# A two-layer perceiver block on one core: where the second half's state-space decays and scan inputs are computed, and the order of the work behind the first layer's attention

## The chip, the cores and the metric

The kernel runs on one core of a Trainium2 chip. The time is the device time of one launch in microseconds (us), as the median of several runs. The core has a matrix engine (TensorE, in the rows PE; PEld is its loading of weights), a vector engine (VectorE, DVE), an activation engine (ScalarE, ACT), a general one (GpSimd, POOL) and a queue that issues transfers (SyncE, SP). They run side by side and meet at semaphores: each takes its instructions strictly in the order in which they are written, so that one waiting instruction holds up everything behind it on its engine.

## What is computed

Two sequences ("halves", b = 0 and 1) of 128 tokens with 256 features pass through six residual steps, each behind a layer norm. The change lies in steps 1 and 2 and the beginning of steps 3 and 4.

```python
x = x + L0_xattn(ln(x), ctx, ctx)       # 16 heads over 2048 keys
x = x + L0_attn(ln(x), ...)             # state-space scan, 16 states per feature
x = x + L0_ffn(ln(x), ...)              # router, low-rank experts ("lora")
x = x + L1_xattn(ln(x), ctx, mask)      # one head over the same 2048 keys
x = x + L1_attn(ln(x), ...)             # 16 heads, compressed and local keys
x = x + L1_ffn(ln(x), ...)              # 8 experts

# the scan of step 2, for each feature d, state n, token t
A      = -exp(A_log)                    # (d, n)
dt     = softplus(x_proj_dt)            # (t, d)
A_bar  = exp(dt[t, d] * A[d, n])        # the decays
u      = dt[t, d] * x[t, d] * B[t, n]   # the scan's input
h[t]   = A_bar * h[t-1] + u
y[t,d] = sum_n h[t, d, n] * C[t, n] + D[d] * x[t, d]
```

## The kernel before, in words

The program is written by hand: each engine has its own list of calls, whose order is the schedule. Everything stays in the core's memory; only weights, contexts and masks are loaded.

Step 1 is a double loop over eight groups of four heads (g = 0 to 3 for the first half, 4 to 7 for the second) and 16 chunks of keys (c). Work of the first half's later steps is put between its pieces by tables named `beside`, one for each engine, keyed by group and chunk. So the first half's scan lies inside the second half's attention, and the second half's scan lies behind it. The semaphore names say what was done: `x_done0` and `x_done1` count the residual steps of a half.

The state space step of one half goes like this. TensorE transposes the normed x (`x_to_columns`, L784) and ScalarE copies it out (`transposed_x`, L503). TensorE projects the step sizes (`step_sizes`, L873), ScalarE copies them (`copy_z`, L543), VectorE takes their magnitude (`step_magnitude`, L1363), ScalarE forms exp and log (L548, L551), VectorE makes dt and dt*x (`step_and_input`, L1368 and L1370, semaphore `dtx_done`). TensorE makes B and C (`state_maps`, L882), VectorE splits them into three bf16 parts (`split_maps`), TensorE spreads each row over 128 partitions (`spread`, L897) in eight pieces of four rows for the second half, and ScalarE copies these out (`bc_copy`, L558, semaphore `bc_sb`); pieces 0 to 3 are B, 4 to 7 are C. The states of 128 features times 16 states times 128 tokens are a tile of 128x2048, and there are two of them for a half (h = 0, 1). For each: exponent dt*A (`decay_exponent`, L1392, on VectorE for the second half), exp (`decay_exp`, L563), input (`state_input`, L394, on GpSimd), scan (L1401), product with C (`read_states`, L1407, semaphore `hc_done`), and a sum over the states in 16 matmuls against the identity (`sum_states`, L905; semaphore `y_ps` when both are done). `add_states` (L1413 to L1416) adds it to x.

Around this lie: `key_mask` (L1468), which turns the loaded mask of 4096 keys into a row of one partition for step 4 and waits for two transfers (mask and bias) that SyncE issues once the first half's `read_states` are both done; `tables` (L1489 to L1499), small products of the rotation tables for step 5; `scores3`, the first half's scores of step 4 (L949, four matmul groups of 512 keys); `max3` (L1473), their maximum; `exp3` (L582); `p3_to_columns` (L960, 16 transposes); `outputs3` (L968, 16 chunks of keys); `add3` (L1482); and `lora_products` (L914, L917), the second half's first matmuls of step 3.

SyncE issues the loads of the projection weights of step 5 when all four `read_states` are done (two of them) and when the second half's sums are done (the third).

Of the kernel before, what the change touches and what calls it, by code (L numbers as in the profile page):

```python
# [18 lines left out]
NB = 2  # L19
# [47 lines left out]
def perceiver_program(nc, io, out):  # L67
    ctx = ExitStack()
    sems = {}
    with ctx:  # L70
# [303 lines left out]
        def _(pool):  # L374
# [50 lines left out]
            state_input(1, 0)  # L425
            state_input(1, 1)
# [65 lines left out]
        def _(sc):  # L492
# [68 lines left out]
            def decay_exp(b, h):  # L561
                sc.wait_ge(S("dta_done"), KD * b + h + 1)
                sc.activation(decay[b][:, h], decay[b][:, h], ACT.Exp, scale=-1.0).then_inc(S("decay_done"), 1)  # L563


# [25 lines left out]
            def state_rates():  # L591
                sc.wait_ge(S("ssm_in"), 32)
                sc.activation(ea[:, :, :], a_log[:, :, :], ACT.Exp).then_inc(S("ea_done"), 1)
# [5 lines left out]
                      (7, 11): [(transposed_x, 2, 0)], (7, 13): [(hidden_exp, 0)]}  # L599
# [82 lines left out]
            weigh_masked(1)  # L682
            gap_exp(0)
            transposed_x(1, 1)
            wxaT(0)
            copy_z(1)
            softplus_exp(1)
            softplus_log(1)
            for i in range(8):
                bc_copy(1, i)  # L690
            transposed_x(3, 0)
            decay_exp(1, 0)
            decay_exp(1, 1)
# [85 lines left out]
        def _(pe):  # L779
# [184 lines left out]
            def outputs3(b):  # L964
                for c in range(NCH):
# [3 lines left out]
                mm.then_inc(S("o3_ps"), 1)  # L969
# [126 lines left out]
            x_to_columns(1, 1)  # L1096
            lora_columns(0)
            step_sizes(1)
            lora_up(0)
            state_maps(1)  # L1100
            for i in range(8):
# [3 lines left out]
            scores3(0, 1)  # L1105
            sum_states(1, 0)
            sum_states(1, 1)
            p3_to_columns(0)
            outputs3(0)
            x_to_columns(2, 1)  # L1110
            lora_products(1)
            x_to_columns(4, 0)
# [165 lines left out]
        def _(ve):  # L1278
# [110 lines left out]
            def decay_exponent(b, h):  # L1389
                ve.wait_ge(S("ea_done"), 1)  # L1390
                ve.wait_ge(S("dtx_done"), b + 1)
                ve.tensor_tensor(decay[b][:, h], dt[b][:, P * h:P * (h + 1)].unsqueeze(1).to_broadcast([P, NS, P]),  # L1392
                                 ea[:, h, :].unsqueeze(2).to_broadcast([P, NS, P]), ALU.mult)\
                    .then_inc(S("dta_done"), 1)

            def scan(b, h):

                ve.wait_ge(S("decay_done"), KD * b + h + 1)
# [11 lines left out]
            def add_states(b):  # L1410
                ve.wait_ge(S("lora_in"), 128)
                ve.wait_ge(S("dta_done"), KD * (b + 1))
# [220 lines left out]
            key_mask()  # L1633
# [8 lines left out]
            lora_weighted(0)  # L1642
            step_magnitude(1)
            split_maps(1)
            lora_add(0)
            ln_stats(3, 0)
            step_and_input(1)
# [205 lines left out]
```

## Time and profile before

| what | value |
|---|---|
| median of 3 runs | 527.75 us (525.65 to 529.73) |
| the profiled execution | 525.38 us, its span 523.4 us |
| busy share of the span | TensorE 82%, VectorE 68%, ScalarE 51%, GpSimd 20% |
| end of the attention of the second half | about 210 us in the span |
| stretch that the change touches | about 191 to 272 us |

The profile's time stamps count from the start of the span. A row of the timeline has start, duration, engine, line, operation, output and inputs, their sizes, how many instructions were merged, and in brackets the idle time before it and who ended it. A page of the profile also has the chain of waits: followed back from the last instruction, at each step to what released it. The granted clock of TensorE is 1.00 (2.4 GHz) or 0.50 (1.2 GHz).

### The profile page before, as it was taken

To read this page: it belongs to the slowest core of one execution; us is meant where nothing else is said; L and a number is where in the kernel's file an instruction comes from. 1 tells how busy PE (TensorE), PEld (TensorE's weight loads), DVE (VectorE), ACT (ScalarE), POOL (GpSimd) and SP (SyncE) were. 2 spreads that over 40 slices of the span, in tenths; PEclk is the share of its full clock that TensorE was granted. 3 is DMA by queue.
4 is the path that set the end of the run, shared out by engine and by line. 5 is a ranking of instruction groups with operands and counts; after the bars stand their busy time and mean duration, and the time that the engine had idled before them with its cause. 6 is when DMAs were issued, how large, how long until landed. Compare 5 with 4: busy or idle time off the path is not lost.

```text
span 523.4 us, 8961 instructions
## 1 busy us (share of the span) xinstructions
PE 429.0 (82%) x3584; PEld 311.1 (59%) x3584; DVE 354.1 (68%) x550; ACT 266.2 (51%) x571; POOL 105.0 (20%) x70
## 2 busy tenths in 40 slices
PE   0177687998787898475989998999789979999997
PEld 0124355665554485332854373444678869999996
DVE  4952977778486965499852838277464499777872
ACT  4314545775758344261313071455785066777762
POOL 4010000001057100073000408025300022333300
PEclk9999978999899599768899998999899989999999
DMA  5599333444230026200560000000930097640000
GB/s 212 141 288 321 122 91 88 113 122 123 70 89 1 1 59 275 51 0 0 209 276 0 2 0 2 0 0 6 360 119 3 0 328 259 218 162 1 2 2 20
DMA packets 27305, 54.11 MB, mean 103 GB/s; under 512 B 5017, under 2 KB 17529, under 8 KB 23930
## 3 DMA queue, kind: packets, MB, share of 16 engines
q1 hardware_dynamic: 27264, 53.54, 32.2%
q8 instruction: 28, 0.46, 0.4%
q14 instruction: 13, 0.11, 0.1%
HBM read 40.65 MB, written 0.26 MB: 78 GB/s over the span
## 4 chain that ended last, share of the span: by engine, by line
PE 55%; DVE 29%; ACT 6%; issue 6%; DMA 2%; POOL 1%; SPq 0%; DVEq 0%; ACTq 0%; POOLq 0%
PE ps L1218 17%; PE ps L1039 8%; DVE mx L1612 7%; PE ps L854 4%; PE ps L810 3%; PE ps L841 3%; DVE reg_b L1401 2%; DVE reg_a L1401 2%; PE ps L1183 2%; DVE reg_a L1313 2%; PE ps L949 1%; ACT reg_b L625 1%; PE ps L1173 1%; PE ps L1172 1%; PE ps L968 1%
## 5 line engine op out<-in xcount | busy, mean ns | idle before, releaser
L1612 DVE TENSOR_REDUCE mx<-ps 128x1 f32<-128x1024 f32 x64 | 76.8, 1221 | 44.3 <-PE ps L810 35.3
L625 ACT ACTIVATE reg_b<-ps 128x512 f32<-128x512 f32 x128 | 75.4, 598 | 46.8 <-PE ps L841 26.8
L841 PE MATMUL ps<-qreg,reg_b 98*128 98x128 bf16 x512 | 50.3, 236 | 4.9 <-ACT reg_b L625 3.7
L1039 PE MATMUL ps<-reg_b,xT 128*128 128x512 f32 x96 | 49.9, 644 | 0.0
L1218 PE MATMUL ps<-part_a 128*128 128x256 f32 x384 | 48.2, 283 | 0.4 <-DVE part_a L1757 0.4
L841 PEld LDWEIGHTS ps<-qreg,reg_b 98*128 98x128 bf16 x512 | 38.2, 106 | 15.8 <-ACT reg_b L625 6.7
L1218 PEld LDWEIGHTS ps<-part_a 128*128 128x128 f32 x384 | 46.9, 192 | 0.6 <-DVE part_a L1757 0.6
L854 PE MATMUL ps<-reg_b 128*32 128x128 f32 x1024 | 47.0, 305 | 0.0
L810 PE MATMUL ps<-reg_b,qreg 96*128 96x512 bf16 x96 | 37.1, 455 | 11.9 <-DVE mx L1612 9.2
L760 ACT ACTIVATE reg_a<-ps,b 128x256 f32<-128x256 f32 x64 | 30.2, 472 | 23.7 <-PE ps L1218 23.6
L1218 PE MATMUL ps<-part_a,part_b 128*128 128x256 f32 x288 | 37.5, 290 | 1.5 <-DVE part_a L1729 0.6
L1757 DVE TENSOR_TENSOR part_a<-reg_a,part_a 128x256 fp32r<-128x256 f32 x64 | 26.4, 439 | 18.1 <-ACT part_a L763 18.1
L634 ACT COPY reg_a<-ps 128x512 f32<-128x512 f32 x24 | 14.0, 586 | 47.9 <-PE ps L1039 47.9
L1218 PEld LDWEIGHTS ps<-part_a,part_b 128*128 128x128 f32 x288 | 36.4, 198 | 2.0 <-DVE part_a L1757 0.7
L377 POOL TENSOR_TENSOR rstd<-ve,cf 128x1 f32<-128x1 f32 x12 | 6.7, 560 | 144.5 <-DVE ve L1291 144.4
L414 POOL COPY reg_b<-reg_a 128x1024 f32<-128x1024 f32 x8 | 8.3, 1041 | 123.5 <-PE ps L863 99.8
L854 PEld LDWEIGHTS ps<-reg_b 128*32 128x32 f32 x1024 | 27.3, 118 | 7.4 <-issue 1.9
L1039 PEld LDWEIGHTS ps<-reg_b,xT 128*128 128x128 f32 x96 | 17.1, 198 | 18.0 <-issue 18.0
L763 ACT CAST part_a<-reg_a 128x256 fp32r<-128x256 f32 x64 | 26.0, 407 | 2.0
L471 POOL CAST part_b<-reg_b 128x1024 fp32r<-128x1024 f32 (+1 forms) x9 | 16.6, 1853 | 47.9 <-PE ps L1218 33.9
L810 PEld LDWEIGHTS ps<-reg_b,qreg 96*128 96x128 bf16 x96 | 8.2, 103 | 27.1 <-DVE mx L1612 17.3
L792 PE MATMUL ps<-cb,oreg 128*96 128x128 bf16 x32 | 3.9, 315 | 24.8 <-DVE oreg L1338 24.8
(278 smaller groups left out, 878.4 us busy)
## 6 DMA issues: line engine op xcount, KB each, us to landing
reg_b<-in_w SPq DMA_DIRECT2D x16, 512.0 KB, 7.6
reg_b<-in_w SPq DMA_DIRECT2D x8, 1024.0 KB, 6.9
reg_b<-reg_b SPq DMA_DIRECT2D x56, 128.0 KB, 2.8
reg_b<-in_w_qkv SPq DMA_DIRECT2D x3, 2048.0 KB, 13.4
reg_b<-reg_a SPq DMA_DIRECT2D x40, 128.0 KB, 2.5
reg_a<-in_ctxK SPq DMA_DIRECT2D x4, 1024.0 KB, 6.8
reg_a<-in_ctx SPq DMA_DIRECT2D x2, 2048.0 KB, 9.7
reg_a<-in_ctxT SPq DMA_DIRECT2D x2, 2048.0 KB, 10.0
```

The costliest lines, as they stand in the source:

```text
L471: pool.tensor_copy(high[e % 2][i], raw[e % RAW][i]).then_inc(S(name), 1)
L625: sc.activation(pT[n % 3], score_b[n % 2], ACT.Exp).then_inc(S("exp_done"), 1)
L760: sc.activation(hid[layer][:, m, :], ps[:, 2 + m, 0:NB * P], ACT.Gelu, bias=(b1, b2)[layer][:, e, m:m + 1]).then_inc(S(f"h{layer + 1}_sb"), 1)
L763: sc.copy(hid_high[layer][:, m, :], hid[layer][:, m, :]).then_inc(S(f"h{layer + 1}_high"), 1)
L810: mm = pe.matmul(score_a[m % 2][:, i, :], q, k, start=True, stop=True)
L841: mm = pe.matmul(cols, kS[g % 3][0:SROWS, c // 8, j, P * (c % 8):P * (c % 8 + 1)], qT[b][0:SROWS, HPG * hg + j, :], start=not last, stop=True)
L854: mm = pe.matmul(ps[VW * j:VW * (j + 1), 7, 0:P], va[g % 2][:, c, j, :], pT[n % 3][:, P * j:P * (j + 1)], start=c == 0, stop=c == NCH - 1)
L1039: mm = pe.matmul(bank(b, n % 2), xT[b][:, i, :], w_qkv[:, j, i, 512 * n:512 * (n + 1)], start=False, stop=i == KD - 1)
L1218: mm = pe.matmul(out, left[u], right[v], start=(i, u, v) == (0, 0, 0), stop=(i, u, v) == (len(terms) - 1, 0, 1))
L1401: link(ve.tensor_tensor_scan(state[b][:, h].rearrange("p n l -> p (n l)"), decay[b][:, h].rearrange("p n l -> p (n l)"), state[b][:, h].re ...
L1612: ve.reduce_max(mx[:, piece // 2, piece % 2:piece % 2 + 1], score_a[m % 2].rearrange("p i k -> p (i k)"), X_AXIS).then_inc(S("max_done"), 1)
L1757: ve.tensor_tensor(hid_low[layer][:, m, :], hid[layer][:, m, :], hid_high[layer][:, m, :], ALU.subtract).then_inc(S(f"h{layer + 1}_low"), 1)
```

## The change

- The second half's decays are computed by ScalarE alone: for each of the two tiles 16 instructions of 128x128, one per state, exp(scale * dt) with the rate of that state as a scale per partition (`decay_by_state`). VectorE's two products for the exponents are gone. The rates are stored negated, by one small copy more in the attention.
- The second half's two scan inputs move from GpSimd to VectorE (`state_input`).
- An exp of one column (`exp_table`) stands on ScalarE right behind the log, so that the table of functions is switched there.
- B and C are spread and copied in two parts: B ahead of step 4's scores on TensorE and ahead of the decays on ScalarE, C behind them.
- VectorE: `key_mask` moves from before `add_states(0)` to behind `lora_weighted(0)`, `step_and_input(1)` ahead of `lora_add(0)`, `tables` ahead of the scans, `max3(0)` ahead of the `read_states`.
- TensorE: `step_sizes(1)` and `state_maps(1)` one place earlier each; `outputs3(0)` is cut in two with `x_to_columns(2, 1)` and `lora_products(1)` between.
- ScalarE: `weigh_masked(1)` moves into the attention's last group, `copy_z(1)` ahead of `wxaT(0)`.

```diff
@@ POOL
-            state_input(1, 0)
-            state_input(1, 1)
@@ ACT
             def decay_exp(b, h):
                 sc.wait_ge(S("dta_done"), KD * b + h + 1)
-                sc.activation(decay[b][:, h], decay[b][:, h], ACT.Exp, scale=-1.0).then_inc(S("decay_done"), 1)
+                sc.activation(decay[b][:, h], decay[b][:, h], ACT.Exp).then_inc(S("decay_done"), 1)
+            def decay_by_state(h):
+                sc.wait_ge(S("dtx_done"), NB)
+                for n in range(NS):
+                    sc.activation(decay[1][:, h, n, :], dt[1][:, P * h:P * (h + 1)], ACT.Exp, scale=ea[:, h, n:n + 1])\
+                        .then_inc(S("decay_done"), 1)
+            def exp_table():
+                sc.activation(small[1][:, 7:8], neg_half, ACT.Exp)
...
-                sc.activation(ea[:, :, :], a_log[:, :, :], ACT.Exp).then_inc(S("ea_done"), 1)
+                link(sc.activation(ea[:, :, :], a_log[:, :, :], ACT.Exp))
+                sc.activation(ea[:, :, :], ea[:, :, :], ACT.Copy, scale=-1.0).then_inc(S("ea_done"), 1)
...
-                      (7, 11): [(transposed_x, 2, 0)], (7, 13): [(hidden_exp, 0)]}
+                      (7, 11): [(transposed_x, 2, 0)], (7, 13): [(hidden_exp, 0)],
+                      (7, 8): [(weigh_masked, 1)]}
...
-            weigh_masked(1)
             gap_exp(0)
             transposed_x(1, 1)
+            copy_z(1)
             wxaT(0)
-            copy_z(1)
             softplus_exp(1)
             softplus_log(1)
-            for i in range(8):
+            exp_table()
+            for i in range(4):
                 bc_copy(1, i)
             transposed_x(3, 0)
-            decay_exp(1, 0)
-            decay_exp(1, 1)
+            decay_by_state(0)
+            decay_by_state(1)
+            for i in range(4, 8):
+                bc_copy(1, i)
             exp3(0)
@@ PE
-            def outputs3(b):
-                for c in range(NCH):
+            def outputs3(b, chunks=range(NCH)):
+                for c in chunks:
...
             x_to_columns(1, 1)
+            step_sizes(1)
             lora_columns(0)
-            step_sizes(1)
+            state_maps(1)
             lora_up(0)
-            state_maps(1)
-            for i in range(8):
+            for i in range(4):
                 spread(1, i)
             x_to_columns(3, 0)
             scores3(0, 0)
             scores3(0, 1)
+            for i in range(4, 8):
+                spread(1, i)
             sum_states(1, 0)
             sum_states(1, 1)
             p3_to_columns(0)
-            outputs3(0)
+            outputs3(0, range(0, 8))
             x_to_columns(2, 1)
             lora_products(1)
+            outputs3(0, range(8, NCH))
             x_to_columns(4, 0)
@@ DVE
-            def decay_exponent(b, h):
-                ve.wait_ge(S("ea_done"), 1)
-                ve.wait_ge(S("dtx_done"), b + 1)
-                ve.tensor_tensor(decay[b][:, h], dt[b][:, P * h:P * (h + 1)].unsqueeze(1).to_broadcast([P, NS, P]),
-                                 ea[:, h, :].unsqueeze(2).to_broadcast([P, NS, P]), ALU.mult)\
-                    .then_inc(S("dta_done"), 1)
+            def state_input(h):
+                ve.wait_ge(S("dtx_done"), NB)
+                ve.wait_ge(S("bc_sb"), 20)
+                ve.tensor_tensor(state[1][:, h], tmp[1][:, h * P:(h + 1) * P].unsqueeze(1).to_broadcast([P, NS, P]),
+                                 bc_row[1][:, 0:NS, :], ALU.mult).then_inc(S("dbx_done"), 1)
...
-                ve.wait_ge(S("decay_done"), KD * b + h + 1)
+                ve.wait_ge(S("decay_done"), h + 1 if b == 0 else KD + NS * (h + 1))
...
             read_states(0, 1)
-            key_mask()
             add_states(0)
...
             lora_weighted(0)
+            key_mask()
             step_magnitude(1)
             split_maps(1)
+            step_and_input(1)
             lora_add(0)
             ln_stats(3, 0)
-            step_and_input(1)
+            state_input(0)
             ln_apply(3, 0)
-            decay_exponent(1, 0)
-            decay_exponent(1, 1)
+            state_input(1)
+            tables()
             scan(1, 0)
+            scan(1, 1)
+            max3(0)
             read_states(1, 0)
-            scan(1, 1)
             read_states(1, 1)
-            max3(0)
-            tables()
             add_states(1)
```

VectorE, from the second half's dt*x to its scans, before (names with 0 and 1 belong to the halves, reg_b is the big buffer that holds decays, states and B and C):

```order
L1370 TENSOR_TENSOR tmp1<-tmpb1,xT 128x256 [waits xT_sb1,dve_step]
L1296 TENSOR_SCALAR xn0<-x0,mv0,rstd0 128x256 [waits ln_rstd0]
L1392 TENSOR_TENSOR reg_b<-tmpb1,ea 128x2048 [waits dtx_done,ea_done] x2
L1399 MEMSET reg_b 128x16 [waits decay_done]
L1401 SCALAR_TENSOR_TENSOR reg_b<-reg_b 128x2048 [waits dbx_done,dve_step]
L1407 TENSOR_TENSOR reg_b<-reg_b 128x2048 [waits bc_sb,dve_step]
L1399 MEMSET reg_b 128x16 [waits decay_done]
L1401 SCALAR_TENSOR_TENSOR reg_b<-reg_b 128x2048 [waits dbx_done,dve_step]
L1407 TENSOR_TENSOR reg_b<-reg_b 128x2048 [waits bc_sb,dve_step]
```

The same place now:

```order
L1385 TENSOR_TENSOR tmp1<-tmpb1,xT 128x256 [waits xT_sb1,dve_step]
L1474 TENSOR_TENSOR x0<-x0,reg_b 128x256 [waits mask_in]
L1476 TENSOR_TENSOR x0<-ps,x0 128x256 [waits lora_ps,dve_step]
L1304 BN_STATS stats0<-x0 128x6 [waits x_done0]
L1305 BN_AGGR mv0<-stats0 128x2 [waits dve_step]
L1306 TENSOR_SCALAR ve0<-mv0 128x1 [waits dve_step]
L1407 TENSOR_TENSOR reg_b<-tmp1,reg_b 128x2048 [waits bc_sb,dtx_done]
L1311 TENSOR_SCALAR xn0<-x0,mv0,rstd0 128x256 [waits ln_rstd0]
L1407 TENSOR_TENSOR reg_b<-tmp1,reg_b 128x2048 [waits bc_sb,dtx_done]
```

The two products L1392 are gone; in their place stand the two scan inputs (L1407 in the new numbering), the first of them ahead of the layer norm xn0 that TensorE and ScalarE need for step 4's scores.

VectorE a little further on, now (L1513 is the last row of `tables`):

```order
L1513 TENSOR_TENSOR qreg<-qreg 8x32 [waits dve_step]
L1413 MEMSET reg_b 128x16 [waits decay_done,dve_step]
L1415 SCALAR_TENSOR_TENSOR reg_b<-reg_b 128x2048 [waits dbx_done,dve_step]
L1413 MEMSET reg_b 128x16 [waits decay_done,dve_step]
L1415 SCALAR_TENSOR_TENSOR reg_b<-reg_b 128x2048 [waits dbx_done,dve_step]
L1487 TENSOR_REDUCE m3_0<-ps 128x1 [waits s3_ps,dve_step]
L1488 TENSOR_SCALAR m3_0<-m3_0 128x1 [waits dve_step]
L1421 TENSOR_TENSOR reg_b<-reg_b 128x2048 [waits bc_sb] x2
```

Both scans now run one after the other, each behind 16 exps of ScalarE, and the maximum m3_0 stands between them and the two products with C, which release the sums on TensorE.

ScalarE, from the second half's softplus to the decays, before:

```order
L551 ACT_TABLE_LOAD
L551 ACTIVATE tmp1<-tmp1 128x256 [waits act_step]
L558 COPY reg_b<-ps 128x512 [waits bc_ps] x8
L503 COPY xT<-ps 128x2x128 [waits xT_ps0]
L563 ACT_TABLE_LOAD
L563 ACTIVATE reg_b<-reg_b 128x2048 [waits dta_done] x2
```

And now, from L546, the exp of the softplus:

```order
L546 ACTIVATE tmp1<-tmp1 128x256 [waits z_abs]
L549 ACT_TABLE_LOAD
L549 ACTIVATE tmp1<-tmp1 128x256 [waits act_step]
L571 ACT_TABLE_LOAD
L571 ACTIVATE small1<-cf 128x1
L556 COPY reg_b<-ps 128x512 [waits bc_ps] x4
L501 COPY xT<-ps 128x2x128 [waits xT_ps0]
L567 ACTIVATE reg_b<-tmpb1,ea 128x128 [waits dtx_done]
L567 ACTIVATE reg_b<-tmpb1,ea 128x128 x15
L567 ACTIVATE reg_b<-tmpb1,ea 128x128 [waits dtx_done]
L567 ACTIVATE reg_b<-tmpb1,ea 128x128 x15
L556 COPY reg_b<-ps 128x512 [waits bc_ps] x4
```

The second table load stands ahead of the copies of B, the 32 exps stand behind four copies and the transposed x of step 4, and the copies of C stand behind the exps.

TensorE at step 4's outputs of the first half, before (L968 is `outputs3`, of which the last two of four parts are shown):

```order
L968 MATMUL ps<-reg_a,reg_b 128x256 [waits p3T_sb]
L968 MATMUL ps<-reg_a,reg_b 128x256 x3
L968 MATMUL ps<-reg_a,reg_b 128x256 [waits p3T_sb]
L968 MATMUL ps<-reg_a,reg_b 128x256 x3
L784 MATMUL ps<-cf,xn1 128x128 [waits xn_done1]
L784 MATMUL ps<-cf,xn1 128x128
L914 MATMUL ps<-xT,oreg 64x128 [waits xT_sb1,lora_in]
L914 MATMUL ps<-xT,oreg 64x128
L917 MATMUL ps<-w_lora,xT 128x256 x2
```

And now, from the second of the four parts:

```order
L979 MATMUL ps<-reg_a,reg_b 128x256 [waits p3T_sb]
L979 MATMUL ps<-reg_a,reg_b 128x256 x3
L795 MATMUL ps<-cf,xn1 128x128 [waits xn_done1]
L795 MATMUL ps<-cf,xn1 128x128
L925 MATMUL ps<-xT,oreg 64x128 [waits xT_sb1,lora_in]
L925 MATMUL ps<-xT,oreg 64x128
L928 MATMUL ps<-w_lora,xT 128x256 x2
L979 MATMUL ps<-reg_a,reg_b 128x256 [waits p3T_sb]
L979 MATMUL ps<-reg_a,reg_b 128x256 x3
L979 MATMUL ps<-reg_a,reg_b 128x256 [waits p3T_sb]
```

Transposes and products of the second half (L795, L925, L928) now stand in the middle of the outputs (L979) instead of behind them.

## Rows read from the trace of the kernel before

**Rows 1.** The page, chain that ended last: its shares of the span by engine.
```profile
PE 55%; DVE 29%; ACT 6%; issue 6%; DMA 2%; POOL 1%; SPq 0%; DVEq 0%; ACTq 0%; POOLq 0%
```

**Rows 2.** Timeline of VectorE: start us, duration us, engine, line, operation, [idle <-releaser].
```profile
195.79 2.28 DVE L1468 TENSOR_SCALAR reg_b<-reg_b 1x4096 bf16<-1x4096 uint8 x1 [4.51 <-DMA reg_b<-in_bias]
...
198.90 0.42 DVE L1416 TENSOR_TENSOR x<-ps,x 128x256 f32<-128x256 f32 x1
```

**Rows 3.** Timeline of TensorE, the same columns, in the attention's last group.
```profile
192.59 3.79 PE L905 MATMUL ps<-cf,reg_a 128*128 128x128 f32 x32
...
201.33 0.44 PE L784 MATMUL ps<-cf,xn 128*128 128x128 f32 x2 [1.09 <-DVE xn L1296]
```

**Rows 4.** Timeline of VectorE, the second half's scan up to step 4's outputs.
```profile
220.30 0.43 DVE L1363 SCALAR_TENSOR_TENSOR tmp<-tmpb 128x256 f32<-128x256 f32 x1 [2.89 <-ACT tmpb L543]
...
225.97 0.42 DVE L1370 TENSOR_TENSOR tmp<-tmpb,xT 128x256 f32<-128x256 f32 x1
...
226.70 8.82 DVE L1392 TENSOR_TENSOR reg_b<-tmpb,ea 128x2048 f32<-128x2048 f32 x2
...
235.60 8.60 DVE L1401 TENSOR_TENSOR_SCAN reg_b<-reg_b 128x2048 f32<-128x2048 f32 x1
244.24 2.29 DVE L1407 TENSOR_TENSOR reg_b<-reg_b 128x2048 f32<-128x2048 f32 x1
...
246.60 4.42 DVE L1401 TENSOR_TENSOR_SCAN reg_b<-reg_b 128x2048 f32<-128x2048 f32 x1
...
253.27 2.28 DVE L1473 TENSOR_REDUCE m<-ps 128x1 f32<-128x2048 f32 x1
...
255.65 0.21 DVE L1489 CAST qreg<-qreg 48x128 bf16<-48x128 f32 x1
...
258.76 0.43 DVE L1413 TENSOR_TENSOR tmpb<-xn,oreg 128x256 f32<-128x256 f32 x1
...
266.88 0.48 DVE L1482 SCALAR_TENSOR_TENSOR x<-ps,m,x 128x256 f32<-128x256 f32 x1 [4.51 <-PE ps L968]
```

**Rows 5.** Timeline of ScalarE, the second half's log, copies of B and C.
```profile
221.20 1.28 ACT L551 ACT_TABLE_LOAD   x1
...
224.31 1.07 ACT L558 COPY reg_b<-ps 128x512 f32<-128x512 f32 x2 [1.41 <-PE ps L897]
225.66 1.08 ACT L558 COPY reg_b<-ps 128x512 f32<-128x512 f32 x2 [0.28 <-PE ps L897]
...
229.34 0.38 ACT L503 COPY xT<-ps 128x256 f32<-128x256 f32 x1
```

**Rows 6.** Timeline of TensorE: sums over the states, transposes and outputs of step 4.
```profile
246.58 6.27 PE L905 MATMUL ps<-cf,reg_b 128*128 128x128 f32 x32 [5.50 <-DVE reg_b L1407]
253.40 3.84 PE L905 MATMUL ps<-cf,reg_b 128*128 128x128 f32 x32 [0.55 <-DVE reg_b L1407]
257.88 1.97 PE L960 MATMUL ps<-cf,reg_b 128*128 128x128 f32 x16 [0.64 <-ACT reg_b L582]
259.69 7.07 PE L968 MATMUL ps<-reg_a,reg_b 128*128 128x256 f32 x32
266.60 0.38 PE L784 MATMUL ps<-cf,xn 128*128 128x128 f32 x2
...
268.08 1.13 PE L917 MATMUL ps<-w_lora,xT 128*128 128x256 f32 x4
```

**Rows 7.** Timeline of GpSimd: the second half's two scan inputs.
```profile
226.88 13.03 POOL L394 TENSOR_TENSOR reg_b<-tmp,reg_b 128x2048 f32<-128x2048 f32 x2 [0.54 <-ACT reg_b L558]
```

**Rows 8.** Timeline of ScalarE in step 5: small instructions back to back.
```profile
374.01 0.31 ACT L741 COPY reg_a<-ps 128x128 f32<-128x128 f32 x1
374.17 0.52 ACT L676 ACTIVATE reg_a<-ps,att,qreg 128x128 f32<-128x128 f32 x1
374.53 0.25 ACT L676 ACTIVATION_READ_ACCUMULATOR reg_a<-ps,att,qreg 128x1 f32 x1
```

**Rows 9.** A stretch: us, busy of PE, PEld, DVE, ACT, POOL, granted clock, DMA.
```profile
246.60:251.60 5.00, 5.00 (x23) 5.00 (x24) 4.96 (x2) 0.00 (x0) 0.00 (x0) 0.50 0.00 0
```

More of the change, by code:

```diff
@@ L968, in outputs3 @@
                     mm = pe.matmul(bank(b, 0, D), p3T[b][:, c, :], ctxN[:, b, c, :], start=c == 0, stop=c == NCH - 1)
-                mm.then_inc(S("o3_ps"), 1)
+                if c == NCH - 1:
+                    mm.then_inc(S("o3_ps"), 1)
             def misc_read(name, count):
@@ L1411, in add_states @@
                 ve.wait_ge(S("lora_in"), 128)
-                ve.wait_ge(S("dta_done"), KD * (b + 1))
+                ve.wait_ge(S("decay_done"), (KD, KD + KD * NS)[b])
                 link(ve.tensor_tensor(tmp2[b][:, :], xn[b][:, :], d_row, ALU.mult))
```

## The prediction

> **What bounds the kernel now.** I read the page first: the chain that ended last lies 55% on TensorE and 29% on VectorE [rows 1], so no single engine is the limit and each stretch has to be read by itself. Then the timelines of the engines, from 191 to 272 us, where the change lies.
>
> In the attention's last group VectorE waits 4.51 us for a transfer, then turns the mask into a row in 2.28 us, and only then makes the first half's x [rows 2]. TensorE had finished the sum that x needs at 192.59 + 3.79 = 196.38, and later waits 1.09 us for the normed x [rows 3].
>
> Behind the attention VectorE is the chain: it waits 2.89 us for the copy of the step sizes, has dt*x ready at 225.97 + 0.42 = 226.39, makes two exponents (8.82 us), scan (8.60), product with C (2.29), scan (4.42), product, maximum (2.28), and from 255.65 to 258.76 the tables [rows 4]. GpSimd runs the two scan inputs from 226.88 to 239.91 meanwhile [rows 7].
>
> From 246.58 TensorE sums the states, then transposes and multiplies for step 4, and ends the outputs at 259.69 + 7.07 = 266.76 [rows 6]. VectorE waits 4.51 us for that and goes on at 266.88 [rows 4]; everything behind hangs on it, since the second half's router stands behind this instruction on VectorE. So **the end of these outputs is what counts**: I work out when it comes, and pass its shift to the end of the kernel one for one.
>
> **The change, part by part**
>
> *Mask row out of the attention.* VectorE would make x at 196.4 instead of 198.90, 2.5 us earlier, but TensorE waits only 1.09 us there; the rest is hidden behind its own work. Gain 1.1 at the end of the attention, with the masked weight of ScalarE moved too and not counted. The 2.28 us come back behind the attention: VectorE stands idle from 217.41 (220.30 less 2.89), in new time 216.3, so it is free at 218.6. The step sizes, now one place earlier on TensorE and ScalarE, are taken to be there by then. Its next instruction, 220.30 before, starts 1.7 earlier.
>
> *Softplus and dt*x.* The table load of the log ran 221.20 to 222.48 [rows 5] and the log behind it takes about 0.4 (a copy of that size 0.38), so to 222.9; now 221.2. dt*x follows directly with two instructions of 0.42 [rows 4]: 222.1, against 226.39. **4.3 us gained so far.**
>
> *The wait for B.* The first scan input on VectorE needs the copies 0 to 3 of B, and these stand behind the new table load of 1.28 us: 221.2 + 1.28 = 222.5, first copy 222.6. Two copies go in 1.08, the next pair starts 224.31 to 225.66 = 1.35 later [rows 5]: 222.6 + 1.35 + 1.08 = 225.0. What VectorE has ahead of it (the x and statistics for step 4) ends sooner: all that it did between 220.30 and 226.39 is 6.1 us, which from 218.6 gives 224.7. So **1.6 to 2.9 of the 4.3 us are lost waiting here**, and behind this instruction are the normed x of step 4, its transposes, its copy on ScalarE and, behind that copy, all decays.
>
> *VectorE from there.* A product of 128x2048 takes 2.29 with GpSimd idle. The exponents took 8.82 / 2 = 4.41 each beside GpSimd, and the first scan 8.60 against 4.42; the 4.31 us from 235.60 to GpSimd's end at 239.91 make 4.42 + 4.31 = 8.73. So a scan stands still while GpSimd runs, and without it all prices are the short ones. Input 225.0 to 227.3, normed x 0.3 (226.39 to 226.70) to 227.6, input to 229.9, tables 3.1 to 233.0, two scans of 4.42 + 0.1 to 242.1, maximum 2.4 (253.27 to 255.65) to 244.5, products with C to 246.8 and 249.1. Before these were at 246.53 and 253.35 (the idle of 5.50 and 0.55 before the sums ends there [rows 6]). **The first is no earlier, the second 4.3 earlier.**
>
> *Under it.* The copy of the transposed x came 0.9 after the normed x (0.38 + 0.38 and hand-overs), 228.5 against 229.72. The scores ran 229.72 to 246.58 - 5.50 = 241.08; now to 240.0, before the maximum at 242.1. The copies of C, two pairs behind that, end at 243.3, before 244.5. The tables wait for small transfers that SyncE issues once the second half's attention is added, which is before 217.41; at 229.9, over 12 us later, I take them as landed. The weights of step 5 start with the fourth product with C, 4 us earlier, which gives nothing, since nobody waits for them.
>
> *The decays.* 32 exps of 128x128 in place of two of 128x2048. No such instruction is in the trace. From below: a plain 128x128 copy is followed by the next instruction after 0.16 (374.01 to 374.17). From above: one with scale and bias per partition and an accumulator is followed after 0.36, and lasts 0.52 by itself [rows 8]. With one operand per partition I take 0.26, the middle. From 228.5: the first 16 at 232.7, all at 236.8. Scan 1 wants them at 233.0, scan 2 at 237.6. So they are **hidden with 0.3 and 0.8 us to spare**; the break-even is (233.0 - 228.5) / 16 = 0.28 each. At 0.16 nothing more is won, at 0.36 the second scan comes 2.4 later, at 0.52 7.5 later.
> The Trainium skill, "ScalarE: Activation LUTs", section "What ACT_TABLE_LOAD costs", gives 186 ns plus 0.833 ns an element, 93 ns for each operand per partition and an overlap of 93 ns. By that, an estimate, one is 0.293 us, 32 are 9.4, and the second scan would come 0.3 us later, 0.3 more on the sum.
>
> *The sums.* The first starts at 246.85, as before. Before it took 6.27 for the work that the second did in 3.84: the granted clock was 0.50 in its first 5 us [rows 9], behind a pause of 5.50. Now TensorE has the four small pieces of C to spread from 240.0 to 243.3 and then a pause of 3.5. Bounds 3.84 and 6.27, I take the middle, 5.1, since the pause is shorter but the work in the pieces thin: 251.95. The second no longer waits for VectorE: **255.8**, where step 4's transposes start, against 257.88. Gain 2.1; the exp for them (released at 244.5) is no longer the last to come.
>
> *The outputs cut in two.* Between their halves now lie transposes, a wait for ScalarE's copy and the products: 266.60 to 268.08 + 1.13 = 269.21, so 2.6 us. Before, this lay behind the outputs, where VectorE needed its time for add and norm anyway. Nobody uses the earlier result: the router's first instruction still stands behind `add3(0)` on VectorE. **Loss 2.6.** Everything else in the diff (negated rates 0.2 us in an attention that ScalarE does not bound, merged waits) costs nothing.
>
> Sum at the outputs' end: - 2.1 + 2.6 = + 0.5, at 267.3 instead of 266.76. The profiled execution's 525.38 becomes 525.9; the median shown, 527.75, lies 2.4 above it, so in medians 528.2. The gains in front are eaten by the wait for B, the mask row, and the cut.
>
> **The rivals**
>
> 1. *The clock stays up in the sums, or is low for the whole of the first one:* 3.84 or 6.27 instead of 5.1, so -1.3 or +1.2. It is the forecast's own spread: 526.9 to 529.4.
> 2. *The clock falls again behind the outputs.* TensorE now has no products left to do there and stands nearly idle for the 4.7 us until the router's logits. A price: once more the difference 6.27 - 3.84 = 2.4. For: the pause is about as long as the 5.50 before the sums. Against: two small pieces lie in it. 530.6.
> 3. *ScalarE becomes the bound of the scans,* slower than before: the exps neither overlap nor get cheaper than 0.52, then the second scan waits until 228.5 + 32 x 0.52 = 245.1, + 7.5, 535.7. It takes over 1% (5.3 us) at (237.6 + 4.8 - 228.5) / 32 = 0.43 each. Against: no back-to-back row has more than 0.36 from start to start, and there with two operands. At 0.36 it is + 2.4, 530.6.
> 4. *The VectorE gain passes through.* If the wait for B is not there (-1.6 to -2.9) and the cut costs little, because what bounded the outputs was the copying of their transposes: the fourth product with C is done at 247.5 or earlier, and the outputs end up to 6.5 earlier, 521.2; with one of the two, 525. For: VectorE is rid of 8.8 + 4.2 us of contended work and gets 4.6 instead. Against: the outputs ran at an even pace in the rows.
>
> **How the numbers follow.** Forecast with its spread 0.55; second fall of the clock 0.14; decays at about 0.36 0.10; above 0.43 0.06; gain passes through 0.15, half of it over 1%. One per cent, 5.3 us, is about what can be told from no change here, since the runs of before alone spread over 4.1 us. Faster by more 0.09 (half of rival 4, and a little for runs that fall well), slower by more 0.09 (the slow decays, and rivals 2 and 3 together), the same 0.82. The range: from 523.5, rival 4 with one of its two parts and some of the runs' spread, to 532.0, rival 2 or the decays at 0.36 with the clock low in the first sum.
>
> **What would show it.** In the changed profile: no wait for a transfer at the mask row; a wait of VectorE for ScalarE's copies before the first scan input; two scans of 4.4; ScalarE's 32 exps start to start 0.26, ended before the second scan; the first sum at about 247 and between 3.8 and 6.3 long; transposes of step 4 at about 256; outputs with a gap of 2.6 in their middle and an end near 267. It is wrong if the outputs end before 264 or after 270, or if the shift at 267 is not the shift at the end.

## The result, and the profile after

The changed kernel takes 530.37 us (median of 20 runs, 526.62 to 532.42), the kernel before 526.49 us in the same session (20 runs, 523.75 to 531.02). The ratio is 1.0065, 95% interval [1.0047, 1.0084]: slower by some 3.4 us. The medians differ by 3.9. The forecast was 528.2 within 523.5 to 532.0, no change by the bound of 1%. That held, but its sum, + 0.5 us, explains only a small part of the loss.

The profiled execution takes 530.91 us, its span 528.9 us, 5.5 us more than before. TensorE's mean granted clock is 0.916 of full speed, before 0.935. The page, chain that ended last, shares by engine, the line that answers to [rows 1]:

```profile
PE 60%; DVE 22%; ACT 10%; issue 5%; POOL 1%; DMA 1%; SPq 0%; ACTq 0%; DVEq 0%; POOLq 0%
```

VectorE gave up 7 points of the chain, issue and transfers one each, and TensorE and ScalarE took 9. Timeline of VectorE, to be laid beside [rows 2] and [rows 4]:

```profile
196.62 0.42 DVE L1430 TENSOR_TENSOR x<-ps,x 128x256 f32<-128x256 f32 x1 [4.42 <-PE ps L916]
...
216.15 2.27 DVE L1482 TENSOR_SCALAR reg_b<-reg_b 1x4096 bf16<-1x4096 uint8 x1
218.35 0.41 DVE L1378 SCALAR_TENSOR_TENSOR tmp<-tmpb 128x256 f32<-128x256 f32 x1
...
221.96 0.42 DVE L1385 TENSOR_TENSOR tmp<-tmpb,xT 128x256 f32<-128x256 f32 x1
...
224.66 2.29 DVE L1407 TENSOR_TENSOR reg_b<-tmp,reg_b 128x2048 f32<-128x2048 f32 x1 [0.62 <-ACT reg_b L556]
226.88 0.41 DVE L1311 TENSOR_SCALAR xn<-x,mv,rstd 128x256 f32<-128x256 f32 x1
...
233.26 0.07 DVE L1413 MEMSET reg_b<- 128x16 f32 x1 [0.79 <-ACT reg_b L567]
233.36 4.42 DVE L1415 TENSOR_TENSOR_SCAN reg_b<-reg_b 128x2048 f32<-128x2048 f32 x1
...
238.04 4.42 DVE L1415 TENSOR_TENSOR_SCAN reg_b<-reg_b 128x2048 f32<-128x2048 f32 x1
242.49 2.29 DVE L1487 TENSOR_REDUCE m<-ps 128x1 f32<-128x2048 f32 x1
...
244.89 4.48 DVE L1421 TENSOR_TENSOR reg_b<-reg_b 128x2048 f32<-128x2048 f32 x2
```

The wait for a transfer at the mask row is gone, and x follows TensorE's sum at once. dt*x ends at 222.38, 4.0 us earlier than in [rows 4], but the first scan input starts 2.3 us behind it: x and its statistics for step 4 stand between, then a wait of 0.62 us for ScalarE's copies of B. Both scans take 4.42 us where the first took 8.60. ScalarE under it, for [rows 5]:

```profile
220.95 1.28 ACT L571 ACT_TABLE_LOAD   x1
...
222.36 2.21 ACT L556 COPY reg_b<-ps 128x512 f32<-128x512 f32 x4
228.06 0.37 ACT L501 COPY xT<-ps 128x256 f32<-128x256 f32 x1 [3.50 <-PE ps L795]
228.33 9.45 ACT L567 ACTIVATE reg_b<-tmpb,ea 128x128 f32<-128x128 f32 x32
```

ScalarE stands idle for 3.50 us in front of the copy of the transposed x, for which VectorE makes the normed x only behind the first scan input. TensorE behind it, for [rows 6]:

```profile
247.23 9.60 PE L916 MATMUL ps<-cf,reg_b 128*128 128x128 f32 x64 [6.36 <-DVE reg_b L1421]
256.67 1.91 PE L971 MATMUL ps<-cf,reg_b 128*128 128x128 f32 x16
258.42 3.62 PE L979 MATMUL ps<-reg_a,reg_b 128*128 128x256 f32 x16
261.87 0.38 PE L795 MATMUL ps<-cf,xn 128*128 128x128 f32 x2
...
264.32 3.62 PE L979 MATMUL ps<-reg_a,reg_b 128*128 128x256 f32 x16
270.55 0.44 PE L795 MATMUL ps<-cf,xn 128*128 128x128 f32 x2 [2.60 <-DVE xn L1311]
271.54 0.60 PE L1069 MATMUL ps<-xT,qreg 128*1 128x128 f32 x4 [0.55 <-ACT xT L501]
272.68 0.61 PE L933 MATMUL ps<-rw,tmp 64*128 64x16 f32 x2 [0.55 <-DVE tmp L1444]
273.22 2.07 PE L936 MATMUL ps<-w_lora,xT 128*128 128x256 f32 x4
...
275.76 3.65 PE L1051 MATMUL ps<-reg_b,xT 128*128 128x512 f32 x4
```

The outputs end at 264.32 + 3.62 = 267.94, 1.2 us later than the 266.76 before. Behind them TensorE now pauses 2.60 us, and then its products run at half speed: four of 128x256 take 2.07 us, the same shape took 1.13 at 268.08 in [rows 6], and four of 128x512 take 3.65. The stretch 272 to 280 of both kernels (us, busy of PE, PEld, DVE, ACT, POOL, granted clock, DMA), before:

```profile
272.00:280.00 8.00, 7.58 (x19) 3.24 (x19) 3.87 (x20) 1.96 (x5) 0.00 (x0) 0.79 0.01 2
```

and after:

```profile
272.00:280.00 8.00, 7.45 (x15) 3.33 (x14) 4.99 (x23) 1.06 (x3) 0.00 (x0) 0.57 0.02 3
```

From the first projection on (its second group of products starts at 277.04 before, 279.66 after) the shift is 2.6 us, and it stays so up to about 375. There the clock falls in both, and stays at 0.50 for longer in the changed kernel (6.8 us against 3.4): + 5.5 at the end.

### The profile page after: what moved, and what is told of

It is laid out like the page before. It is cut to its first block, busy times and chain, and to the rows that moved or that the text cites. A ratio compares the mean times of both kernels' runs of the same rounds, so it can differ in the third digit from the quotient of the medians.

```text
span 528.9 us, 8990 instructions
## 1 busy us (share of the span) xinstructions
PE 432.6 (82%) x3584; PEld 314.5 (59%) x3584; DVE 345.8 (65%) x550; ACT 272.0 (51%) x603; POOL 91.6 (17%) x68
## 4 chain that ended last, share of the span: by engine, by line
PE 60%; DVE 22%; ACT 10%; issue 5%; POOL 1%; DMA 1%; SPq 0%; ACTq 0%; DVEq 0%; POOLq 0%
PE ps L1233 17%; PE ps L1051 9%; DVE mx L1626 6%; PE ps L865 5%; PE ps L852 4%; PE ps L821 3%; PE ps L916 3%; PE ps L1198 2%; ACT reg_b L567 2%; DVE reg_a L1328 2%; ACT reg_b L634 2%; PE ps L1188 2%; PE ps L1187 2%; PE ps L960 1%; DVE reg_a L1415 1%
## 5 line engine op out<-in xcount | busy, mean ns | idle before, releaser
L852 PE MATMUL ps<-qreg,reg_b 98*128 98x128 bf16 x512 | 51.4, 239 | 4.9 <-ACT reg_b L634 3.7
```

Source lines behind the costliest of these rows:

```text
L852: mm = pe.matmul(cols, kS[g % 3][0:SROWS, c // 8, j, P * (c % 8):P * (c % 8 + 1)], qT[b][0:SROWS, HPG * hg + j, :], start=not last, stop=True)
```

## The experiments

Every kernel was timed against the kernel before on the same chip; that one's medians were 526.06 us beside experiments 1 to 4, 526.78 beside 5, 6, 7 and 9, and 527.0 beside 8, 10 and 11. The changed kernel itself was timed apart from them, against 526.49; distances to its 530.37 us are read together with the ratios. In the traces milestones are counted from T, the start of TensorE's transposes of the second half's normed x behind the attention, since T itself moves by up to 2.7 us between executions. The changed kernel has T = 214.51, sums over the states from T + 32.72, outputs' end seen by VectorE (L1496) at T + 53.55, second projection group at T + 65.15; before, T = 215.69, 30.89, 51.19 and 61.35. Each trace is one execution: in three of them (the changed kernel, experiments 9 and 10) the code up to the outputs' end is the same, the sums start at T + 32.72 in all three, and still take 9.60, 10.19 and 10.12 us, so that the outputs' end moves by 0.6 us by itself.

**1. The changed kernel with its outputs in one piece.**

```diff
-            outputs3(0, range(0, 8))
+            outputs3(0)
             x_to_columns(2, 1)
             lora_products(1)
-            outputs3(0, range(8, NCH))
```

> The changed kernel with step 4's outputs of the first half uncut again, the second half's transposes and products behind them as before the change. Theory A (the cut costs): the outputs end 2.6 us earlier, at 265.3 instead of 267.9 in the span, and VectorE's add with them. The kernel gains 2.6 us or a little more, since the products again fill TensorE's pause behind the outputs: about 1.5 us below the kernel before. Rival B (TensorE's clock alone makes it slower, the cut is free): the outputs end within 0.5 us of 267.9 and the time stays that of the changed kernel.

Measured: 523.25 us (12 runs), ratio 0.9921 [0.9889, 0.9953], 7.1 us under the changed kernel. Outputs seen at T + 51.17, 2.4 us earlier; second projection group at T + 59.73, 5.4 earlier. The stretch 272 to 280 of its trace:

```profile
272.00:280.00 8.00, 7.58 (x24) 3.38 (x23) 4.29 (x19) 1.65 (x4) 0.00 (x0) 1.00 0.01 1
```

So the cut costs its own 2.4 us and 3.0 more in the clock up to the projection; the rest of the 7.1 comes later. Without the cut the change is a gain, of 2.8 us in the medians. But counted from T its outputs end where they did before (51.17 against 51.19): what VectorE was relieved of has not reached them. The gain is found in the attention's earlier end (1.3, see experiment 6) and in the projection, whose second group starts 1.6 earlier than before, at the full clock.

**2. The kernel before with the cut alone**, the same edit the other way round.

> The kernel before with one edit: outputs cut in two, the second half's transposes and products between. Theory A: the outputs end 2.6 us later, 269.4 instead of 266.8, and behind them TensorE has a pause of about 2.6 to 3 us with nothing to do before the next transposes; time + 2.6 us, and up to 1.5 more where the projections behind run at the lower clock: ratio 1.005 to 1.008. Rival B: + 0 to 1.5 us, from the clock alone.

Measured: 531.01 us (10 runs), ratio 1.0102 [1.0067, 1.0138], + 5.0. Outputs at T + 53.59 (+ 2.4), second projection group at T + 64.47 (+ 3.1), granted clock 0.57 in 272 to 280. The cut alone makes more than the whole loss, though the trace places only 3.1 of the 5.0.

**3. The normed x ahead of the first scan input.**

```diff
-            state_input(0)
             ln_apply(3, 0)
+            state_input(0)
             state_input(1)
```

> The changed kernel with the first half's norm for step 4 ahead of the first scan input on VectorE, so that the transposed x and the decays on ScalarE no longer stand behind the wait for B. Theory C (the decays gate the first scan only by their late start): they start at about 226.2 instead of 228.3, and are done by 235.7; the first scan no longer waits 0.79 us for them; everything on VectorE comes 0.8 us earlier, the sums start at 246.4 instead of 247.2; time - 0.8 us. Rival D (VectorE is the chain and 0.79 is all other engines' slack): no change at all at the sums, because the first scan then waits for something else.

Measured: 528.1 us (12 runs), ratio 1.002 [0.9994, 1.0046], 2.3 us under the changed kernel. The decays start 2.4 us earlier, counted from T, and no longer hold back the scan; the sums start at T + 31.99, 0.7 earlier. The outputs are seen at T + 52.06, 1.5 earlier, but the other 0.8 is the sums' own length, 8.84 us against 9.60.

**4. The maximum behind the products with C.**

```diff
-            max3(0)
             read_states(1, 0)
             read_states(1, 1)
+            max3(0)
```

> The changed kernel with the maximum of step 4 behind the two products with C instead of ahead of them. Theory E (the sums on TensorE are the bound there, and they wait for the first product with C, which the maximum delays): the first sum starts 2.3 us earlier, at 244.9, the transposes of step 4 too (exp of step 4 is released at 249.5 and done by 251.6, before the sums end); time - 2.3 us, and up to 2 more if TensorE's clock stays up, its pause ahead of the sums being 4 us instead of 6.4. Rival F (what comes after the maximum on ScalarE is the bound): the transposes start where they did, time 0.

Measured: 527.54 us (12 runs), ratio 1.0006 [0.9977, 1.0035], - 2.8. Its row of the sums:

```profile
246.40 9.65 PE L916 MATMUL ps<-cf,reg_b 128*128 128x128 f32 x64 [3.45 <-DVE reg_b L1421]
```

They start at T + 30.33 instead of 32.72, the outputs are seen at T + 51.20: the 2.4 us of the maximum pass through in full, since the exp it releases is hidden under sums of 9.65 us.

**5. The second table load behind the copies of B.**

```diff
-            exp_table()
             for i in range(4):
                 bc_copy(1, i)
+            exp_table()
```

> The changed kernel with the exp of one column, which loads the table, behind the four copies of B instead of ahead of them. ScalarE waits 3.5 us behind those copies anyway. The copies start at 221.0 to 221.6 instead of 222.4, VectorE's wait of 0.62 us before the first scan input goes. Theory I (a chain of VectorE up to the sums): everything from there 0.6 us earlier, the 0.79 us wait for the decays stays, time - 0.6 us. Rival (no effect): the wait before the input stays, from another cause.

Measured: 528.9 us (12 runs), ratio 1.0048 [1.0019, 1.0076], - 1.5, with an interval that overlaps the changed kernel's. VectorE waits 0.24 us for the copies instead of 0.62, and still 0.79 for the decays; the sums start 0.5 earlier, at T + 32.21. The outputs are seen at T + 52.28, 1.3 earlier, and again the rest is the length of the sums, 8.84 us.

**6. The mask row back in the attention.**

```diff
+            key_mask()
             add_states(0)
 ...
             lora_weighted(0)
-            key_mask()
```

> The changed kernel with the mask row back ahead of the first half's add, as in the kernel before. Forecast by its own step: TensorE waits about 1.1 us for the normed x in the attention's last group again, the end of the attention comes 1.1 us later; behind it VectorE has 2.28 us less to do before the step sizes' magnitude, but that then waits for the copied step sizes, so 0.5 us or less comes back. Time + 0.6 to + 1.1 us against the changed kernel. Rival (the move was free of effect, because the 2.28 us only changed their place): 0.

Measured: 530.87 us (12 runs), ratio 1.0091 [1.0053, 1.0129], + 0.5. From the start of TensorE's sum for the first half in the attention (192.72) to T it takes 23.15 us, in the kernel before 23.10, in the changed kernel and in experiments 9 and 10 21.78 to 21.79: the row costs 1.4 us there, and TensorE waits 1.30 us for the normed x again. Behind T nothing comes back for it: VectorE waits 2.01 us for the step sizes instead of making the row, and the sums start at T + 32.85 against 32.72. The times cannot tell whether 0.5 or the whole 1.4 arrives at the end, since the two intervals overlap ([1.0053, 1.0129] and [1.0047, 1.0084]).

**7. Edits 1, 3, 4 and 5 together.**

> The changed kernel with four edits together: outputs uncut, the first half's norm ahead of the scan inputs, the maximum behind the products with C, the table load behind the copies of B. If they add: the sums start 0.7 + 0.6 + 2.3 earlier, the outputs end 2.5 (uncut) + 0.7 + 1.5 to 2.5 earlier than in the changed kernel; 3 us below the uncut one, ratio to the kernel before 0.985 to 0.989. If the sums on TensorE or its clock eat the earlier start: as the uncut one, 0.992.

Measured: 521.1 us (6 runs), ratio 0.9879 [0.9835, 0.9923]. It beats both kernels, the one before by 1.2%. Outputs at T + 48.35.

**8. The scan inputs back on GpSimd**, the rest of the change as it is.

```diff
@@ POOL
+            state_input(1, 0)
+            state_input(1, 1)
@@ DVE
-            state_input(0)
             ln_apply(3, 0)
-            state_input(1)
```

> The changed kernel with the second half's two scan inputs back on GpSimd; everything else stays, so VectorE's only other work there is the normed x and the tables. Theory (a scan of VectorE stands still while GpSimd multiplies two inputs): GpSimd runs from about 224.7 to 224.7 + 2 x 4.4 or more = 233.8 or later, the normed x is done 2.3 us earlier (225.4), the decays end at about 235.6, the first scan starts at 229.5 to 230 beside GpSimd and is stretched by their overlap, ending at 238 to 240, the second at 243 to 244.5: the products with C end within 1.5 us of the changed kernel's, the median is the same, 530 within 1.5. Rival: the move of the inputs to VectorE is what the change lives on, GpSimd's products take the 6.5 us each that they did beside the exponents, the first scan ends at 242 or later and the second at 247: 534 or more.

Measured: 533.48 us (6 runs), ratio 1.0136 [1.0093, 1.0178], + 3.1. GpSimd first, then VectorE, in its trace:

```profile
224.94 9.12 POOL L394 TENSOR_TENSOR reg_b<-tmp,reg_b 128x2048 f32<-128x2048 f32 x2 [0.18 <-ACT reg_b L558]
```

```profile
225.12 4.54 DVE L1505 CAST qreg<-qreg 48x128 bf16<-48x128 f32 x1
229.70 4.51 DVE L1506 TENSOR_TENSOR qreg<-qreg 48x128 f32<-48x128 f32 x1
234.25 0.22 DVE L1507 CAST qreg<-qreg 48x128 bf16<-48x128 f32 x1
...
236.94 4.42 DVE L1417 TENSOR_TENSOR_SCAN reg_b<-reg_b 128x2048 f32<-128x2048 f32 x1
```

The time is near the rival's 534, and the reason is neither's. GpSimd's two products take 4.56 us each, not 6.5; it is VectorE that stands still, and not in a scan. A cast of 48x128, which takes 0.21 us elsewhere, ends with GpSimd's first product, and the next small one with its second. The tables took 11.6 us instead of 3.1, and the scan started 3.3 later, counted from T. This is what [rows 4, 7] showed at the first scan (8.60 us beside 4.31 of GpSimd), in its plainest form.
By the Trainium skill, "SBUF — State Buffer", section "Who interferes with whom", VectorE and GpSimd share a pair of ports to the core's memory under an exclusive lock: a VectorE instruction with two inputs in this memory, or a cast in a two-port mode, is blocked until the GpSimd instruction that came first ends. The two rows agree: 4.54 and 4.51 us beside two GpSimd products of 4.56. In which mode the cast ran no run here shows.

**9. Nine useless 128x128 products in TensorE's pause behind the outputs** (nobody reads their result).

```diff
             outputs3(0, range(8, NCH))
+            for i in range(9):
+                pe.matmul(bank(0, 1, P), xT[1][:, 0, :], ident, start=True, stop=True)
             x_to_columns(4, 0)
```

> The changed kernel, cut kept, with nine products of 128x128 of no use put into TensorE's pause of 2.6 us behind the outputs (9 x 0.24 = 2.1 us of added work, results unread, nobody waits for them). Theory G (half of the cut's price is the clock: TensorE is idle behind the outputs, and the router's logits and the first projection then run at 1.2 GHz): the outputs end as in the changed kernel, the logits' and first projection's matmuls take 1.1 and 2.0 us instead of 2.1 and 3.65; time - 2 to - 4 us although work is added. Rival H (the clock falls at this place whatever TensorE does): same rows as the changed kernel, time within 0.5 us of it.

Measured: 528.18 us (12 runs), ratio 1.0026 [0.9998, 1.0054]. The pause went from 2.60 to 0.59, but the clock fell all the same, 1.2 us later (0.50 from about 273.5), and the projection was as slow as in the changed kernel: its stretch of 272 to 280 has 0.60, the second projection group starts 7.10 us behind the logits, 6.98 in the changed kernel. Filling the longest pause alone does not keep the clock up. So the median, which meets the lower end of theory G's forecast, does so by chance: its 2.2 us must lie elsewhere, if they are there at all, since the intervals overlap. In this one trace the clock does not fall at 327, where the changed kernel's does.

**10. As 9, with ten products, and two more in each of the next two gaps of 0.55 us.**

```diff
+            for i in range(10): ...
             x_to_columns(4, 0)
+            for i in range(2): ...
             block_scores(0)
+            for i in range(2): ...
             lora_logits(1)
```

> The changed kernel plus fourteen useless 128x128 products on TensorE, whose result nobody reads: ten in its pause of 2.6 us behind the outputs, two each in the two gaps of 0.55 us behind the next transposes and the next small products. Theory (TensorE's thin work from the end of the outputs to the router's logits is what brings the clock down there): with nine products in the pause alone it still fell, 1.2 us later; with the two next gaps full as well it stays at 1.00 until at least 280, the router's products and the first projection take 1.13 and 1.98 us instead of 2.07 and 3.65, about 2.6 us less, the median 527.5. Rival: the fall has its cause earlier, in the gap of the cut or the thin work before the outputs, and filling behind them is useless: granted clock 0.50 from about 273.5 again, median within 0.7 of the one with nine products, 528.2, or above it by the 0.5 us that the added ones delay.

Measured: 527.09 us (12 runs), ratio 1.0011 [0.9987, 1.0035]; the ratio is 0.0054 under the changed kernel's, 2.8 us, and the two intervals don't meet. Its trace from the added products on (the rows count each of these products twice):

```profile
271.03 2.39 PE L1128 MATMUL ps<-cf,xT 128*128 128x128 f32 x20
273.80 0.44 PE L795 MATMUL ps<-cf,xn 128*128 128x128 f32 x2 [0.37 <-DVE xn L1317]
274.07 0.61 PE L1131 MATMUL ps<-cf,xT 128*128 128x128 f32 x4
274.79 0.60 PE L1069 MATMUL ps<-xT,qreg 128*1 128x128 f32 x4
275.32 0.71 PE L1134 MATMUL ps<-cf,xT 128*128 128x128 f32 x4
275.96 0.39 PE L933 MATMUL ps<-rw,tmp 64*128 64x16 f32 x2
276.28 1.13 PE L936 MATMUL ps<-w_lora,xT 128*128 128x256 f32 x4
...
277.66 1.98 PE L1051 MATMUL ps<-reg_b,xT 128*128 128x512 f32 x4
```

The products behind the logits take 1.13 and 1.98 us, and the second projection group follows the logits by 3.93 us, as in the uncut kernel (3.94), instead of 6.98. In all eight traces that have the cut and not this filling, the distance is 6.25 to 7.10 us, in the three of uncut changed kernels 3.93 or 3.94, so this is hardly one lucky execution. The granted clock is 1.00 in all of 264 to 375. So work that computes nothing, put where the cut had left TensorE nearly idle, gives back the 3.0 us that the clock cost there, and the 2.4 of the cut itself stay. From T to the end this execution is 2.7 us shorter than that of experiment 9; their medians lie only 1.1 apart, with intervals that overlap, so the traces tell the two apart and the times do not.

**11. Edits 1, 4 and 5, without the normed x first.**

> The changed kernel with three orders altered: outputs in one piece, maximum behind the products with C, second table load behind the copies of B; the first scan input stays ahead of the normed x. Against the kernel with all four altered (521.1) this leaves out the normed x first. If the parts add, it is 0.5 to 1.5 us slower than that: 521.5 to 522.5. Rival: the normed x first gives nothing, since the decays it starts earlier are not waited for once the table load is out of the way of B: 521 or below.

Measured: 521.11 us (6 runs), ratio 0.9884 [0.9841, 0.9928], the same as with all four. The rival's time is right: with B no longer behind the table load, next to nothing is left for the earlier normed x (outputs at T + 48.48 and T + 48.35). Its reason is not: VectorE still waits 0.79 us for the decays here. With the normed x first it waits 0.67 us for GpSimd's part of that norm instead, and the first scan starts at T + 18.19 there and T + 18.27 here.

## Why the prediction was right and where it failed

*Mask row out of the attention: - 1.1.* From the first half's sum to T it takes 1.3 us less, and putting the row back cost 1.4. The 2.28 us are spent behind the attention, at 216.15, and VectorE is free for its next instruction at 218.35 where 218.6 was said; with the row back it only waits there. Right; how much of it arrives at the end the times do not tell (experiment 6).

*dt*x at 222.1, the wait for B, first input at 225.0.* Measured 222.38, a wait of 0.62 us for the copies, 224.66. Right. Experiments 3 and 5, which take away what is queued behind this wait or most of the wait itself, bring the sums 0.7 and 0.5 us forward; of their 2.3 and 1.5 us in the medians the rest is not placed by this.

*The decays, 0.26 each, hidden with 0.3 to spare.* They took 9.45 / 32 = 0.295 us, above the break-even of 0.28, and VectorE waited 0.79 us for the sixteenth at 233.26; of that 0.3 is late against the 233.0 of the sum. The second scan did not wait. The row nearest in form would have been the upper of the two, with its operand per partition. The estimate worked out from the Trainium skill, "ScalarE: Activation LUTs", section "What ACT_TABLE_LOAD costs", was 0.293, and the measurement agrees with it.

*VectorE's prices without GpSimd.* Products 2.29, scans 4.42, maximum 2.4: all as taken. Products with C done at about 247.1 and 249.4 against 246.8 and 249.1. Experiment 8 shows the cause, as far as GpSimd is concerned.

*The sums, 5.1 + 3.84 = 8.94.* They took 9.60; the clock is 0.54 in their first 5 us. The pause in front of them is 6.36 us and not 3.5, but that is not the reason: experiment 4 has the pause as it was forecast and 9.65, experiment 11 a pause of 3.19 and 9.95, and experiment 3 the longest pause and sums as short as any:

```profile
249.09 8.84 PE L916 MATMUL ps<-cf,reg_b 128*128 128x128 f32 x64 [8.01 <-DVE reg_b L1421]
```

Taking the middle of 3.84 and 6.27 because the pause is shorter was no way to this number; what sets it stays open. Start 0.4 late, duration 0.7 over: transposes at 256.67 instead of 255.8. So - 1.2 instead of - 2.1, and all of the 1.2 is the attention's earlier end: they start at T + 42.16, before at T + 42.19. The second product with C came 2.8 us earlier from T, but the first 1.8 later, behind both scans and the maximum, and TensorE has the same work behind it. That is why experiment 4 is worth its full 2.4.

*The cut, + 2.6.* Seen by VectorE it is + 2.4 in both directions (experiments 1 and 2), so outputs' end at 267.94 where 267.3 was said. Right in kind and size.

**The step that failed** is the sentence that the shift at the end of the outputs passes to the end of the kernel one for one. In the traces it is + 1.2 at the outputs, + 2.6 from the projection to 375 and + 5.5 at the end, + 3.9 in the medians; by the prediction's own last sign this part is wrong. What came on top of the sum is first of all rival 2, given 14%: the clock falls behind the outputs. Its price of 2.4 us was near, against the same kernel without the cut it is 3.0, and against the kernel before, which lost some clock there too (0.79 in 272 to 280), 1.4. The argument against it, that two small pieces lie in the pause, was wrong in a way that experiments 9 and 10 show: it is not the pause of 2.6 us by itself, but the thin work up to the logits with it. The chain from the outputs' end to the logits is 4.7 us of small instructions on VectorE, GpSimd and ScalarE, and the cut took the transposes and products away that had kept TensorE at work beside them.

So what was worked out for the stretch holds within 0.7 us, and the change as a whole is a gain of 2.8 us (experiment 1: 523.25 against 526.06) with a loss of 7.1 in two moved lines. The forecast weighed the second as + 2.6.

That the time fell into the range is in part luck. The forecast was + 0.5 us and the medians moved by + 3.9. It was counted from 527.75, the median of the first three runs, and that of twenty is 526.49: from there the sum would have said 527.0 for the measured 530.37. The range held because its upper end was drawn for rival 2 or the slow decays.

*Rival 4*, that VectorE's gain passes through, has a real part: the changed order without the cut can give some 6 us (experiments 7 and 11 against before), here reached only with the orders of 4 and 5 together.

What stays open is the last part of the loss. Of the 7.1 us between the changed kernel and the uncut one, 5.4 are placed; the rest lies behind 280, where single traces have the clock falling at about 325 to 330 (before and changed) or not at all (experiments 1, 9 and 10), and for 3.4 or 6.8 us at 375. One execution of each kernel doesn't tell whether the change brings that or whether it falls so by chance. The 2 us of experiment 9 are of the same kind.

## What to carry to other kernels

Before moving matmul work out of the place where TensorE would otherwise wait for a chain of small instructions, look at the granted clock behind that place, and price the next big products at half speed. Work moved earlier is only worth something if somebody reads it earlier; ask for each moved piece what its engine does in the place that it left. An instruction that releases only hidden work (the maximum) goes behind one that releases visible work.

## What the runs showed of the hardware

- Fourteen 128x128 products whose result nobody reads, put between the end of the outputs and the logits, made the changed kernel faster by 2.8 us (ratio 1.0011 against 1.0065). Nine in the longest pause alone left the clock at 0.50 from 273.5.
- A VectorE cast of 0.21 us took 4.54 us and a product of 48x128 4.51 us beside GpSimd's 128x2048 product, while that took 4.56 us (4.55 in the first half's scan inputs before, at 161.52). Beside VectorE's own products of 128x2048, GpSimd's took 13.03 / 2 = 6.5 [rows 7].
- A 128x128 exp with a scale per partition follows the one before it after 0.295 us, so 32 of them take 9.45 us, where one exp over 128x2048, the columns of sixteen, took 1.91 in the kernel before:

```profile
231.03 1.91 ACT L563 ACTIVATE reg_b<-reg_b 128x2048 f32<-128x2048 f32 x1
```

  ScalarE pays 5.6 us more so that VectorE is rid of two products of 4.41 [rows 4].
